# Four transformer layers on one core: halves for the queries of the fourth attention, and the shared expert's down products summed unit by unit

## The reference, cut to what matters

```python
x = x + _L3_xattn_ref(_layernorm(x, axis=-1), ctx_2048, Wq, bq, Wkv, bkv, Wp, bp)
x = x + _L3_ffn_ref(_layernorm(x, axis=-1), router_w, w1, w2, w_gate, w_up, w_down)

# attention: 16 heads of 16; q, k and v are rounded to whole multiples of a scale
q = fq_sym((x @ Wq + bq) / 4, per head row); k, v likewise
attn = softmax(q @ k.T); attn = fq_unsigned(attn)      # multiples of max/255
out = (attn @ v) @ Wp + bp

# feed-forward: 8 experts of 512, top 2 of them for each token, and a shared expert of 1024
logits = x @ router_w;  top 2 -> scores = softmax(top_logits)
routed = sum over the 2: score * ((silu(g) * u) @ w2[e]),  g, u = split(x @ w1[e])
shared = (silu(x @ w_gate) * (x @ w_up)) @ w_down
return routed + shared
```

## Time and profile before

| | |
|---|---|
| median of the timed runs | 1105.83 us (3 runs, 1105.2 to 1108.23) |
| profiled execution, own time | 1113.83 us |
| its span, first to last instruction | 1112.1 us |
| mean granted TensorE clock | 0.865 of 2.4 GHz |
| PE busy | 919.5 us, 83% |
| DVE busy | 620.2 us, 56% |
| ACT busy | 526.3 us, 47% |
| POOL busy | 252.4 us, 23% |
| scores of the fourth attention (line 2244) | first at 647.7 us, last at 828.6 us |
| feed-forward part of the fourth layer | 859.9 us to the end |

### The profile page before, as it was taken

One profiled execution on the slowest core, in us unless ns is written; L12 is line 12 of the kernel. 1 busy time (PEld: TensorE's weight loads), 2 busy tenths in 40 slices (PEclk: granted clock), 3 DMA queues, 4 the chain that ended last, 5 costly groups with the idle time before them and its releaser, 6 DMA issues. The chain is left out here.

```text
span 1112.1 us, 15443 instructions
## 1 busy us (share of the span) xinstructions
PE 919.5 (83%) x5390; PEld 539.1 (48%) x5416; DVE 620.2 (56%) x1304; ACT 526.3 (47%) x794; POOL 252.4 (23%) x297
## 2 busy tenths in 40 slices
PE   5698987998998548799799467787866978999996
PEld 2244435666487324444357423333435454666654
DVE  4577755445345875745456579999985411111123
ACT  3166664222423665578643169898982102222210
POOL 4010100000000001313542127667771230000031
PEclk9599999899899869999899765655567899999999
DMA  3613301000357004667144547878650021111022
GB/s 123 155 35 74 110 15 47 1 1 1 127 65 80 0 1 121 184 162 129 44 189 83 196 86 150 162 150 185 108 91 13 24 71 29 41 45 48 24 59 70
DMA packets 130445, 91.64 MB, mean 82 GB/s; under 512 B 92805, under 2 KB 119631, under 8 KB 128591
## 3 DMA queue, kind: packets, MB, share of 16 engines
q1 hardware_dynamic: 125522, 83.45, 33.4%
q0 software_dynamic: 1536, 4.20, 1.2%
q10 hardware_dynamic: 3312, 3.02, 0.8%
HBM read 56.09 MB, written 15.86 MB: 65 GB/s over the span
## 5 line engine op out<-in xcount | busy, mean ns | idle before, releaser
L2270 ACT ACTIVATE sb_l_E<-PS,sb_l_NB,sb_L3SQS 128x1024 uint8<-128x1024 f32 x128 | 154.4, 1207 | 22.7 <-DVE sb_l_NB L2304 13.0
L2301 DVE TENSOR_REDUCE sb_l_NM<-PS 128x1 f32<-128x1024 f32 x128 | 155.5, 1215 | 5.3 <-PE PS L2244 5.3
L2244 PE MATMUL PS<-sb_l_K,sb_l_Q 128*128 128x512 bf16 x232 | 115.4, 589 | 40.9 <-ACT sb_l_E L2270 33.1
L2209 POOL CAST sb_l_ET<-sb_l_EP 128x1024 bf16<-128x1024 uint8 x128 | 128.5, 1040 | 79.0 <-DMA sb_l_EP<-sb_l_E 77.3
L613 DVE TENSOR_REDUCE sb_negmax<-PS 128x2 f32<-128x512 f32 x128 | 84.1, 690 | 31.6 <-PE PS L463 31.4
L2254 PEld LDWEIGHTS PS<-sb_L3VI,sb_l_ET 128*128 128x128 bf16 x1024 | 54.8, 112 | 72.5 <-issue 46.8
L1368 PE MATMUL PS<-sb_L3w,sb_block_xT 128*128 x184 | 83.0, 594 | 4.5 <-DVE sb_hidden L1458 3.0
L599 ACT ACTIVATE sb_E<-PS 128x1024 f32<-128x1024 f32 x64 | 65.4, 1023 | 42.2 <-PE PS L526 42.2
L923 ACT ACTIVATE sb_E<-PS 128x1024 f32<-128x1024 f32 x64 | 65.3, 1024 | 24.6 <-PE PS L830 20.9
L463 PE MATMUL PS<-sb_K,sb_Q 96*128 96x256 bf16 x256 | 53.9, 302 | 15.9 <-ACT sb_negmax_T L573 10.3
L1458 DVE TENSOR_TENSOR sb_hidden<-sb_hidden,PS 128x512 f32<-128x512 f32 x23 | 15.8, 688 | 88.2 <-ACT sb_hidden L1423 88.2
(11 more groups left out here) (336 smaller groups left out, 1720.9 us busy)
## 6 DMA issues: line engine op xcount, KB each, us to landing
sb_Q<-q SPq DMA_DIRECT2D x48, 192.0 KB
sb_L3w<-L3w SPq DMA_DIRECT2D x16, 512.0 KB, 6.7
sb_K<-k SPq DMA_DIRECT2D x24, 192.0 KB
sb_W2E<-L3w SPq DMA_DIRECT2D x8, 512.0 KB, 4.7
q<-sb_q_parts SPq DMA_DIRECT2D x12, 256.0 KB, 4.0
xs<-zero_row SPq DMA_DIRECT2D x1, 2944.0 KB, 47.9
sb_block_x<-xs SPq DMA_DIRECT2D x23, 128.0 KB, 2.2
ys<-sb_block_y ACTq DMA_DIRECT2D x23, 128.0 KB, 2.4
```

The lines of the kernel that those rows point to most:

```text
L2209: return eng.tensor_copy(ET[:, u % CRING], EP[:, u // 2 % TRING, :, :, u % 2])
L2244: ins = pe.matmul(core.bank(2 * (n % SRING) + half), Q[:, h % RING, t * P:(t + 1) * P], K[:, h % RING, half * HALF:(half + 1) * HALF], sta ...
L2270: act.activation(E[:, n // 2 % ERING, :, n % 2], S(n), ACT.Exp, bias=NB[:, n:n + 1], scale=scale_of(h, t), accum_out=ZS[:, n:n + 1]).then_ ...
L2301: dve.tensor_reduce(NM[:, n:n + 1], S(n), axis=AX.X, op=ALU.max, negate=True).then_inc(maxed, 1)
```

## The change

In `attention_l3`, `load_q` takes a range of tokens. The first half of the queries of the four heads is sent as soon as its copy is out (`out_a` at 1), with 12 DMAs of 512 tokens, and the second half with 12 more, on a semaphore of its own, `q_late`. PE starts its `WARM` products between the turns of the two halves, and starts scores without waiting for the second half; unit 2 waits for both copies (it writes the banks that they read), unit 4 for `q_late`. ACT loads its table after its first copy. The last unit, 127, is cast by DVE.

In `moe_silu` the shared expert's down products are made per unit: `shared_part(n)` adds the share of unit n for four token tiles, into two banks that stay open for the whole half (6 and 7 for half 0, 6 and 4 for half 1); two tiles share a bank. DVE adds a whole bank of two tiles at once (`add_shared`), for half 1 after all merges. Hidden parts are kept for two units only. Blocks are turned two ahead instead of one. POOL scatters all tokens by their first choice when `SLOT[0]` is written (`placed` at 1), then by the second, and no longer waits for `EB`.

```diff
-            chain(dve.tensor_copy(SLOT[k][:, :], SF[:, :]))
+            dve.tensor_copy(SLOT[k][:, :], SF[:, :]).then_inc(placed, 1)
+            dve.wait_ge(placed, k + 1)
...
-            pool.wait_ge(routed, 1)
             pool.wait_ge(core.xs_cleared, 16)
-            for t in range(NT):
-                for k in range(2):
+            for k in range(2):
+                pool.wait_ge(placed, k + 1)
+                for t in range(NT):
...
+            def shared_part(n):
+                kind, half, k = units[n]
+                pe.wait_ge(hidden, n + 1)
+                if half and k == 0:
+                    pe.wait_ge(h_out, BLOCKS)
+                    pe.wait_ge(x_out, BLOCKS)
+                for t in range(4):
+                    ins = pe.matmul(core.PS[:, SHARED_BANKS[half][t // 2], t % 2 * D:(t % 2 + 1) * D],
+                                    HS[:, k % 2, t * P:(t + 1) * P], WD[:, k, :], start=(k == 0 and t % 2 == 0), stop=(k == SC - 1 and t % 2 == 1))
+                    ins.then_inc(shared_down, 1)
...
-            for n in range(NU + 2):
+            for n in range(NU + 1):
                 if n < NU:
                     go_up(n)
                 if n == 1:
                     pe_counts(pe)
-                if 1 <= n <= NU and units[n - 1][0] == "block":
+                if n >= 1 and units[n - 1][0] == "shared" and n != SC:
+                    shared_part(n - 1)
+                if n == SC - 1:
+                    shared_part(n)
+                    turn_x(0)
+                    turn_x(1)
+                if n >= 1 and units[n - 1][0] == "block":
                     turn_hidden(units[n - 1][2])
-                for d in downs_at[n]:
-                    if d[0] == "shared":
-                        go_down(*d)
-                if n + 1 < NU and units[n + 1][0] == "block":
-                    turn_x(units[n + 1][2])
-                for d in downs_at[n]:
-                    if d[0] == "block":
-                        go_down(*d)
+                if n < NU and units[n][0] == "block" and units[n][2] + 2 < BLOCKS:
+                    turn_x(units[n][2] + 2)
+                if 2 <= n and units[n - 2][0] == "block":
+                    go_down(units[n - 2][2])
...
+            def add_shared(half, pair):
+                dve.wait_ge(shared_down, 4 * SC * (half + 1) - 2 + 2 * pair)
+                X = core.X[:, 4 * half + 2 * pair:4 * half + 2 * pair + 2, :].rearrange("p t d -> p (t d)")
+                if half:
+                    dve.wait_ge(merged, 2 * NT)
+                dve.tensor_tensor(X, X, core.bank(SHARED_BANKS[half][pair]), ALU.add).then_inc(x_added, 1)
...
-                if n == NU - SC + 7:
+                if n == NU - 2:
+                    dve.wait_ge(x_added, 2)
                     for t in range(4):
                         merge(t)
+                if n == NU - 1:
+                    for t in range(4, NT):
+                        merge(t)
+            for pair in range(2):
+                add_shared(1, pair)
...
-    by_pool = [True for u in range(NU)]
+    by_pool = [u != NU - 1 for u in range(NU)]
...
+                sp.wait_ge(out_a, 1)
+                for h in range(RING):
+                    load_q(h, slice(0, HALF), q_in[h])
                 sp.wait_ge(out_a, 2)
                 for h in range(RING):
-                    load_q(h)
+                    load_q(h, slice(HALF, TOK), q_late)
...
-                pe.wait_ge(out_a, 2)
-                pe.wait_ge(out_v, 2)
-                for i in range(WARM):
-                    pe.matmul(core.bank(7), core.identb[:, :], VI[:, 0:2, :].rearrange("p t d -> p (t d)"),
-                              start=True, stop=True)
+                    for i in range(WARM if half == 0 else 0):
+                        pe.matmul(core.bank(7), core.identb[:, :], VI[:, 0:2, :].rearrange("p t d -> p (t d)"),
+                                  start=True, stop=True)
                 for n in range(NU + LAG):
                     if n < NU:
                         h, t = units[n]
                         if t == 0:
                             pe.wait_ge(q_in[h % RING], 16 * (PARTS + 1) * (h // RING + 1))
+                        if h == 0 and t == NT // 2:
+                            pe.wait_ge(q_late, 16 * PARTS * RING)
+                        if n == 2:
+                            pe.wait_ge(out_a, 2)
+                            pe.wait_ge(out_v, 2)
```

More of the change, by code:

```diff
@@ L1276, in moe_silu @@
     block_unit = lambda b: SC + b
[L1277 to L1284 removed]
+    shared_index = lambda n: n if n < SC else n - BLOCKS
+    SHARED_BANKS = ((6, 7), (6, 4))
     XRING, YRING = 4, 3
@@ L1317, in _ @@
                 pool.wait_ge(y_stored[r], 16 * ((BLOCKS - 1 - r) // YRING + 1))
[L1318 removed]
+            pool.wait_ge(down, BLOCKS)
             for t in range(NT):
@@ L1474, in _ @@
-                if n == NU - SC + 7:
+                if n == SC - 1:
+                    for pair in range(2):
+                        add_shared(0, pair)
+                if n >= 2 and units[n - 2][0] == "block":
+                    b = units[n - 2][2]
+                    dve.wait_ge(down, b + 1)
+                    if b >= YRING:
+                        dve.wait_ge(y_stored[b % YRING], 16 * (b // YRING))
+                    dve.tensor_copy(YB[:, b % YRING, :], core.PS[:, 7, 0:D]).then_inc(y_out, 1)
```

110 lines of the change are left out of this document (49 added, 61 removed).

## The result

| | before | changed |
|---|---|---|
| median of the timed runs | 1107.11 us (11 runs, 1105.2 to 1110.32) | 1101.16 us (11 runs, 1094.38 to 1104.46) |
| ratio, 95% interval | | 0.9933, 0.9912 to 0.9954 |
| profiled execution: own time, span | 1113.83, 1112.1 us | 1097.42, 1095.7 us |

The timed runs say 6 us faster by their medians (7.4 by the ratio), the two profiled executions 16.4 us. The prediction said 19.4. Most of what follows is about that spread, so the measure has to be one that the noise ahead of the change doesn't enter. I cut each trace at four instructions: SP's first K load of the fourth attention, DVE's read of the last router's logits, the first turn of a block, and the first up product of half 1 (by its weight load, 0.2 us ahead of the product).

What follows compares the result with a forecast made beforehand. DVE was taken to bound the attention and PE the feed-forward part, which is not full at both ends. Terms 13.1 + 6.6 + 0.65 - 0.9 = 19.4 us, off 1105.83 us, gave 1086.4 us; range 1082.5 to 1091.5 us.

Steps and rivals of the forecast that it cites:

- Half 0: Shared expert's first half: PE reaches the first block at 908.8 instead of 919.02 us, 10.2 us earlier.
- half 1: Shared expert's second half to the kernel's end: 51.3 us against 57.9 us before, 6.6 us saved.
- nothing in the terms depends on that, so I take the 19.4 us from the median: Whole kernel: profiled execution 8.0 us above the timed median, yet 19.4 us subtracted from the median 1105.83 us.
- the late addition comes back: Rival, shared expert's down products: DVE's 3.3 us late addition recurs; 1087.7 to 1093 us, typically 1090; chance 0.15.
- Start of the blocks: First blocks: turning two ahead removes 3.0 us of waits and 0.2 us more, less 0.3 us for a second turn.
- Start of the attention: Fourth attention's start: DVE starts early, then stalls 5 us before its fifth maximum; 0.9 us lost.
- Last cast: Fourth attention's end: second cast on DVE beside POOL's, only PE's 0.4 us following the first; 0.65 us saved.
- The 0.35 us: Fourth attention's end: saving if DVE's and POOL's casts exclude each other; the sum would be 0.3 us worse.
- Earlier scatter: POOL's scatter in half 0: starts 2.7 us earlier, worth nothing by itself because half 0 hides it.
- clock: Rival, both halves: PE's mixed stream granted 1.2 GHz; 20 us more if about 40 us are affected; chance 0.03.
- gather: POOL's gather in half 1: hidden, 2.3 us ahead of DVE's need; scatter-or-gather rival 1088.7 to 1092.4 us, chance 0.06.

Runs made afterwards that it cites:

- e9: The changed kernel run again with nothing altered; 1103.24 us, ratio 0.987 against the kernel before on that chip.
- e10: The kernel before run again, unaltered, on the same chip as e9; 1117.33 us (11 runs).
- e7: e3 with blocks turned one unit ahead, as before, instead of two; 1099.31 us, ratio 0.9859 against the kernel before.
- e3: The changed kernel with only head 0's queries sent in halves, the other three heads whole; 1092.49 us, ratio 0.9865 against the kernel before.
- e8: e3 with POOL's scatter started only after all routing, in the old tile-by-tile order; 1099.89 us, ratio 0.9859 against the kernel before.
- e16: The kernel before run again, unaltered, on the same chip as e17; 1110.83 us (11 runs).
- e4: The changed kernel run again for a second profile; 1097.78 us, ratio 0.991 against the kernel before.
- e5: The kernel before run again, unaltered, for its profile; 1114.82 us (9 runs).
- e12: The changed kernel with eight of the sixteen gathers, each token's second expert left out; 1101.54 us, ratio 0.9862 against the kernel before.
- e13: The kernel before with 8 indirect DMAs each in scatter and gather, second expert left out; 1106.51 us, ratio 0.9902 against the kernel before.
- e15: The changed kernel with the attention's last unit cast by POOL again; 1106.46 us, ratio 0.9889 against the kernel before.
- e1: The kernel before with only the changed fourth attention, old feed-forward part; 1110.93 us, ratio 1.0028 against the kernel before.
- e17: e3 with DVE's merges of tiles one unit earlier; 1094.62 us, ratio 0.9873 against the kernel before.

## Why the prediction was wrong

The sign was right, the size was not. By its own steps:

- **Half 0, 10.2 us; half 1, 6.6 us.** These failed, on the side of the kernel before: what they took as its time was not its usual time. The addition at 904.69 us and what follows it in the earlier trace rows were counted as a property of the old order; they are the hold, 5 us in each half. Without it the old B is 49.1 and the old D 53.2 us, so the terms are 5.1 to 5.6 and 1.75 us. Where it is present, on the same chip, they are 8.0 (e9, e10) and 3.9 us. It does not always cost the old half 0 the same: B is 50.7, 51.5 and twice 54.05 us in the four held profiles.
- **"nothing in the terms depends on that, so I take the 19.4 us from the median".** This is the step at fault. The 8.0 us between the profiled execution and the timed median were a sign that the two were not alike. The first profile is of the held kind; the timed runs of before that came with it (1105.2 to 1110.3 us) lie with those of the two chips seen to be quick (medians 1108.96 and 1110.83), not of the three held sessions (1114.82, 1117.33, 1117.73). That they were quick is argued from this, not shown; the changed kernel's profile beside them is quick. From a quick base the same working would have given 9.8 us for the feed-forward part (the forecast's 227.4 us for B to D against 237.1 to 237.4), 9.6 us in all and 1096.2 us. The changed kernel's median was 1101.16 us. Of the 5.0 us between, 1.3 are the median of before, which moved from 1105.83 to 1107.11 us with more runs; for the rest the runs give no cause, and 9.6 us lies just inside the interval of the timed gain (5.1 to 9.7).
- **The rival "the late addition comes back"** was the right reading of a held chip: the changed kernel pays 3.6 us there (it said 3.3, or 1.3 behind the merges), only in half 1, because in e9's half 0 the late silu (911.4 us, 2.1 us behind its up products) still comes 3.1 us before PE ends the last up products (914.5), and in half 1 (1090.6 us) only 0.7 us before (1091.3). It had 0.15. Its other branch, a held first profile against a quick timing, I did not think of.
- **Start of the blocks, 2.9 us:** 3.6 us in every pair; e7 gives 3.5 for the second turn ahead.
- **Start of the attention, -0.9 us:** measured -0.9 to -1.0, with the stall's place and its releaser as forecast. Its size was 6.5 us, not 5, since DVE's first maximum came 5.7 us earlier after the K load (12.0 against 17.7), not 4.2: the warm products were taken as 0.43 us each, though the row has 11 in 4.27 us, and the second half's turn, forecast 0.5 us later, came no later. The two cancel in the net, because the 24th DMA sets its end. e3 shows the cause: the number of issues.
- **Last cast, 0.65 us:** measured 0.22. I took the two casts as independent. The row shows POOL's cast stretched by 0.5 us beside DVE's 0.69. The Trainium skill ("SBUF — State Buffer", Who interferes with whom) says that a DVE cast in a 2-port mode and a GpSimd instruction exclude each other. The 0.35 us that had been worked out by it is nearer to the measured 0.22 us than my value; whether DVE was in that mode no row shows.
- **Earlier scatter, 0; clock; gather:** right. e8 loses nothing, half 1 runs at 1.00, and the merges on a quick chip do not wait.

From the K load on (A to D) the changed kernel is 10.7 or 8.6 us shorter on a quick chip (471.8 in e16, 461.1 in its first profile, 463.2 in e4) and 15.4 us on a held one (e10, e9). The ratios of the timed runs are 7.4 us (5.1 to 9.7) and 10.0 us (6.5 to 13.5) there, and 14.5 us (11.2 to 17.8) here. Two stretches whose code the change doesn't touch add to the spread. One is ahead of it all: from the first router to the K load it took 430.5 to 432.0 us in ten of nineteen profiles and 434.1 to 435.9 us in nine, with either kernel. The other lies behind the attention's last reciprocal, up to the last router: 26.3 to 26.5 us in all seven profiles with the old attention; with the new one 26.0 to 26.7 us in five and 27.6 to 27.8 us in seven. In those seven the router's 32 products ran at a granted clock of 0.50 (1.2 GHz). The timeline of the changed kernel's first profile (granted clock 0.70 from 864 to 869 us), and of e4 (0.50 from 864 to 871 us):

```profile
864.04 5.19 PE L1187 MATMUL PS<-sb_L3router,sb_XT 128*128 128x8 f32 x32 [1.03 <-PEq L180]
```

```profile
864.69 6.97 PE L1187 MATMUL PS<-sb_L3router,sb_XT 128*128 128x8 f32 x32 [1.03 <-PEq L180]
```

This is most of the 2 us between the two values of A for the changed kernel (234.5 to 234.7 and 236.3 to 236.8). The prediction had no term for it: it saw the clock of the two halves as the only one that the change could move. Why the new attention has it and the old one doesn't was not tested.

## What to carry to other kernels

When a profiled execution lies outside the range of the timed runs, find the stretch in which it differs before any term is taken from it; a wait whose releaser is unnamed is the first suspect. On chips without the hold a stage's length between two fixed instructions repeats here to 0.1 us (C, D) or 0.6 us (B), where the timed runs of one kernel lie up to 10 us apart, so judge edits by stages and profile the old kernel again on the same chip. Small DMAs cost their issue (0.63 us each here, at half the bytes too): send in pieces only what is needed first. And leave a unit's work between a product and its consumer while POOL has a long row of indirect DMAs in flight.

## What was not expected of the hardware

- In four sessions (the first profile of before, e5 to e8, e9 to e12, e13 to e15), PE's completions were seen up to 4.7 us late towards the end of a row of 16 indirect DMAs by POOL, 6.6 us with 20, and not with 8; in the other three (the first profile of the changed kernel, e1 to e4, e16 and e17) never with 16. The DMAs' own completions were not late: SP's first load followed the last scatter's issue by 2.41 to 2.44 us in all. Within one session the kind never changed. What makes a chip one or the other stays open. The trace itself has a second sign of the kind: of the 39 completions of up products in the feed-forward part, 1 to 4 have no record in each of the twelve profiles of the held sessions (2 in e13, where ACT went on 0.04 us behind each), and none is missing in the seven others.
- After waits of 2.3 to 3.8 us that the hold made, PE's next products ran in part at 1.2 GHz (granted clock 0.57 and 0.75 in the two windows); after waits of 0.5 to 1.4 us in the same place they did not.
